# Dealing the edge-count steps of a GNN kernel out anew between the units of its first two dense passes

## What is computed

```
agg  = segment_sum(h[src], dst)              # for every node: sum over its incoming edges
mean = agg / max(deg, 1)
out  = h @ W_self + mean @ W_neigh + b       # relu after the first layer
```

## Time and profile before

| | us |
|---|---|
| median of 3 runs | 1588.9 |
| lowest, highest | 1588.17, 1589.18 |
| the profiled execution, whole | 1588.72 |
| its span, first to last instruction | 1586.6 |
| TensorE busy (matmul) | 1574.5 (99%) |
| VectorE busy | 868.7 (55%) |
| ScalarE busy | 438.6 (28%) |
| GpSimd busy | 140.1 (9%) |

### The profile page before, as it was taken

One profiled execution on the slowest core, in us unless ns is written; L12 is line 12 of the kernel. 1 busy time (PEld: TensorE's weight loads), 2 busy tenths in 40 slices (PEclk: granted clock), 3 DMA queues, 4 the chain that ended last, 5 costly groups with the idle time before them and its releaser, 6 DMA issues.

```text
span 1586.6 us, 22947 instructions
## 1 busy us (share of the span) xinstructions
PE 1574.5 (99%) x7718; PEld 1332.5 (84%) x7720; DVE 868.7 (55%) x1601; ACT 438.6 (28%) x780; POOL 140.1 (9%) x278
## 2 busy tenths in 40 slices
PE   8999999999999999999999999999999999999998
PEld 7777777888888888889989899898998888888886
DVE  8677766464014124564434334343343788888868
ACT  3336554121102001122313123131231233333256
POOL 1351377000000000010000000000001000000000
PEclk9999999999999999999999999999999999999999
DMA  8323344685335545576203012021122333333222
GB/s 305 132 97 134 116 154 161 239 292 206 111 107 182 186 173 183 175 231 236 80 27 106 31 75 79 26 106 34 71 79 106 107 119 119 119 119 119 95 91 50
DMA packets 55974, 205.44 MB, mean 129 GB/s; under 512 B 5392, under 2 KB 14110, under 8 KB 50372
## 3 DMA queue, kind: packets, MB, share of 16 engines
q1 hardware_dynamic: 53204, 190.71, 34.0%
q0 software_dynamic: 2688, 13.63, 2.5%
HBM read 153.85 MB, written 51.52 MB: 129 GB/s over the span
## 4 chain that ended last, share of the span: by engine, by line
PE 95%; DVE 2%; issue 1%; DMA 1%; ACT 0%; SPq 0%; DVEq 0%; ACTq 0%
PE bank L1632 27%; PE bank L1765 27%; PE bank L1784 25%; PE bank L1714 11%; PE bank L1562 2%; PE bank L1606 2%; PE bank L1822 1%; DVE lif_a L1523 0%; DVE w L1259 0%; DMA w_raw<-w_neigh 0%; DMA w_landing<-w_self 0%; DVE lif_b L1523 0%; DMA pr_raw<-w_proj 0%; DVE y L1503 0%; DVE lif_c L1516 0%
## 5 line engine op out<-in xcount | busy, mean ns | idle before, releaser
L1632 PE MATMUL bank<-w,xt 128*128 128x512 f32 x1920 | 467.1, 396 | 0.7 <-DVE xt L1247 0.6
L1765 PE MATMUL bank<-x2t,fc_w 128*128 128x384 f32 (+1 forms) x2304 | 438.4, 350 | 0.6 <-ACT relu L1019 0.6
L1765 PEld LDWEIGHTS bank<-x2t,fc_w 128*128 128x128 f32 x2304 | 411.7, 188 | 25.8 <-issue 0.9
L1632 PEld LDWEIGHTS bank<-w,xt 128*128 128x128 f32 x1920 | 351.9, 188 | 69.8 <-DVE xt L1247 0.8
L1784 PE MATMUL bank<-pr_w,hid 128*128 128x512 f32 (+1 forms) x1728 | 394.8, 389 | 0.0
L1784 PEld LDWEIGHTS bank<-pr_w,hid 128*128 128x128 f32 (+1 forms) x1728 | 320.6, 186 | 70.8
L1473 DVE TENSOR_TENSOR y<-y,bank 128x512 f32<-128x512 f32 (+1 forms) x144 | 98.7, 686 | 207.0 <-PE bank L1784 207.0
L1014 ACT ACTIVATE pr_w<-pr_raw 128x1024 fp32r<-128x1024 f32 x64 | 67.1, 1049 | 366.2 <-PE bank L1784 363.0
L1714 PE MATMUL bank<-z,at 128*128 128x512 f32 x720 | 168.4, 392 | 0.0
L1714 PEld LDWEIGHTS bank<-z,at 128*128 128x128 f32 x720 | 133.9, 188 | 27.3
L1416 DVE TENSOR_TENSOR square<-relu 128x384 f32<-128x384 f32 (+1 forms) x96 | 56.8, 592 | 144.2 <-ACT relu L1019 144.2
(11 more groups left out here) (156 smaller groups left out, 1026.7 us busy)
## 6 DMA issues: line engine op xcount, KB each, us to landing
fc_raw<-w_fc SPq DMA_DIRECT2D x64, 512.0 KB, 4.3
pr_raw<-w_proj SPq DMA_DIRECT2D x64, 512.0 KB, 3.5
xt<-xt_dram SPq DMA_DIRECT2D x24, 1024.0 KB, 5.0
xt_dram<-xt SPq DMA_DIRECT2D x18, 1024.0 KB, 4.4
at<-at_dram SPq DMA_DIRECT2D x18, 640.0 KB, 6.0
part_dram<-rows SPq DMA_DIRECT2D x20, 512.0 KB, 4.0
rows<-part_dram SPq DMA_DIRECT2D x20, 512.0 KB, 4.3
rows<-x SPq DMA_DIRECT2D x17, 512.0 KB, 5.1
```

The lines of the kernel that those rows point to most:

```text
L1632: ins = nc.tensor.matmul(bank[:, 2 * (u % 2) + q, :], xt[j][:, a, k, :], w[:, k, b, q * HALF:(q + 1) * HALF], start=(k == 0 and m == 0), s ...
L1765: ins = nc.tensor.matmul(bank[:, 4 + (c if g == 0 else j % 2), 0:n], fc_w[:, j % 2, k, a, :], x2t[g][:, k, v, c0:c0 + n], start=(k == 0 an ...
```

## The change

The number of steps per unit and their first product are changed, and the third count store's place.

```diff
-A0_STORES = (6, 7, 9)
+A0_STORES = (6, 7, 8)
...
-        [(A0 + 3, 1, 30, 12)] + [(A0 + n, 5, 12, 36) for n in range(4, TILES - 1)] + [(A0 + 9, 3, 12, 24), (S0, 3, 36, 12)]
-        + [(S0 + p, 7 if p in (4, 6, 8) else 8, 0, 48) for p in range(1, TILES)]):
+        [(A0 + 3, 1, 30, 12)] + [(A0 + n, 6, 9, 39) for n in range(4, TILES - 1)] + [(A0 + 9, 5, 9, 35)]
+        + [(S0 + p, 8 if p in (2, 9) else 7, 0, 48) for p in range(1, TILES)]):
```

## The result

| | before | after |
|---|---|---|
| median of 11 runs, us | 1588.71 | 1592.82 |
| lowest, highest | 1587.35, 1589.66 | 1591.65, 1593.62 |
| profiled execution, whole | 1588.72 | 1591.65 |
| its span | 1586.6 | 1589.5 |
| G0's first product, from the span's start | 279.14 | 282.19 |

The ratio of the times is 1.0026, 95% interval [1.0019, 1.0034]: slower by 4.1 us, where 1.4 us was forecast and 0.91 was given to a change under 3.2 us. The measured time lies outside the range of 1587.9 to 1592.1. The profiled execution shows 2.9 of the 4.1.

The account below looks back on a forecast made before the run. TensorE, busy 99% of the span, was taken as the bound, so only its work and waits count. -0.74 + 0.75 + 1.7 - 0.3 = +1.4 us gave 1590.3 us, range 1587.9 to 1592.1 (own range 1589.0 to 1591.5).

Parts of the forecast that it names:

- Light units, +0.75: A0+4 to A0+7, second step at product 15: VectorE's one-hots come late, waits of 0.15 and three of 0.2 us.
- The rival that named reads in A0: Range reads at product 28 of light units collide with 1 MB stores: +3.5 us, 1593.8; chance 0.06.
- A0+8, +1.7: A0+8, second hot step at product 15: TensorE waits 1.7 us for VectorE's one-hots; bounds 0 and 2.5.
- S0's first step, -0.74: S0: the 0.74 us wait for one-hots behind VectorE's last low half of W_self goes.
- A0+9 and the weights, 0: A0+9 into S0: W_self slices still come in time, costing nothing, with 1.35 us of margin.
- Reads in S0, -0.3: S0+5 to S0+7: waits behind slow register reads fall from 1.55 to 1.30 us, about -0.3.
- Steps cost the same wherever they stand: A0 and S0: step prices don't depend on the distance between steps; their sum changes by zero.
- nothing behind G0's start changes: Stages after G0's start keep their lengths; G0's start moves by the forecast sum.
- signs of being wrong: VectorE finishing before product 15 of A0+8, or a difference in a stage behind G0's start.
- the 0.1 to 0.3 named for A0+5 to A0+7: Sign expected if right: TensorE idle 0.1 to 0.3 us ahead of product 15 in these units.

Follow-up runs that it names:

- hot_at_22: Changed kernel with range reads ahead of the step's waits and A0+8's steps before products 9, 22, 28, 34, 40, 46: 1588.60 us, ratio 1.0002.
- keys_first: Changed kernel with early range reads and, from A0+4, the second step's one-hots made before the next tile's rows' low half: 1587.38 us, ratio 0.9994.
- two_in_s0: Changed kernel with three steps in A0+9 and two again in S0 (products 36, 42): 1592.87 us, ratio 1.0031.
- the second profile: The changed kernel unaltered, run once more for another profile: 1592.69 us.

## Why the prediction was wrong, step by step

- **Light units, +0.75: wrong, and this is the step that failed.** "Now it comes at product 15: 15 x 0.229 + 0.88 + 0.27 = 4.59", against one-hots "ready at 4.79". Both times came out (4.6 and 4.83). The step asked only when the one-hots are ready. It left out that an even window's range read stands on TensorE's queue behind the wait for the head keys, and that in each light unit the step at product 15 is an even window. The slack before was not 0.83 but 0.4: in the kernel before's A0+8 the keys come at 119.15, the read runs from 119.32 to 119.65, and the loop's branch ends at 119.98. The last head product could have followed at about 120.04 and came at 120.46. The place moved 0.92 ahead and the keys came 0.22 later: 0.92 + 0.22 - 0.42 = 0.72, and 0.70 was measured in A0+7; in A0+4 to A0+6 the read took 0.6 and not 0.33. Measured 3.78. With the read moved away 1.63 is left, with an odd window 1.32; so 2.1 to 2.5 is the read. The rest is late keys and one-hots with the loop's arithmetic and branch behind them, about twice the forecast; windows with two loop chunks wait 0.6 and not 0.2.
- **The read had been seen, and priced in the wrong stage.** The prediction read the earlier trace rows as a matter of slow transfers in S0 and took reads of 0.333 as free in A0. The rival that named reads in A0 put them at product 28, with the worst length. Product 28 shows no wait: one of the four reads there was slow (0.92, in A0+5), and its lead of 1.3 covered it. Nor does each light unit store 1 MB, as the rival has it: the last such store is issued at 95.04, in A0+6. The reads that cost were of 0.33 and 0.60, at product 15. That the time came near that rival's 1593.8 is luck: it came by another mechanism.
- **A0+8, +1.7: right in kind and nearly in size.** 1.07 at product 15 and 0.36 at the transposes, 1.43. hot_at_22 and keys_first remove the 1.07 in two different ways. The 0.36 was not foreseen: the transposes of tile 9 wait for norm 9 itself, which ended at U + 1.63 (forecast 1.80).
- **S0's first step, -0.74: right.** The wait is gone, and two_in_s0 brings 0.44 of it back.
- **A0+9 and the weights, 0: right.** The margin was 1.7 (forecast 1.35).
- **Reads in S0, -0.3: right in sign, too small.** 1.99 (the small ones counted) fell to 0.56 or 1.03. S0+7, priced at 0.65, costs 0 and 0.20; S0+5 costs 0.27 and 0.41. The prediction looked at the third step of S0+5 to S0+7 alone: S0+8 waited 0.36 at product 20 before and, with the same steps, nothing and 0.13 after; S0+9's third step is an even window too, and S0+4 got a new 0.18. Such waits can't be priced to half a microsecond from one profile. This error of -1.1 hid a part of the +3.0 in the light units.
- **Steps cost the same wherever they stand: right,** to 0.2 us by the 214.6 to 215.0 above, as is that nothing behind G0's start changes.
- **The sum:** -0.74 + 3.78 + 1.43 - 0.07 - 1.43 = 2.97 in the profile, where 1.4 was forecast. Of the medians' 4.1 this leaves 1.1 that no profile shows. The profiled execution was the fastest run of the changed kernel both times. The 1.1 isn't explained. The waits in A0 repeat too well for it. What does vary is the start of A0's first unit, 9.6 to 11.6 us into the span over the thirteen profiles, ahead of everything that the edits touch. That this stretch holds the 1.1 isn't shown, since only one execution of each run is profiled.
- **What the signs missed.** None of the prediction's signs of being wrong appeared. They watched A0+8 and the stages behind G0's start. Only the 0.1 to 0.3 named for A0+5 to A0+7, where 0.96, 0.96 and 0.70 stand, points at the failed step.

## What to carry to other kernels

When work is moved earlier on a queue, the time at which it is wanted is not that of the first big operation but that of the first item in its own chain, and register reads, range arithmetic and branches behind a wait belong to that chain. Look at whether such a read stands behind a wait that it doesn't need: moving it ahead of the wait took a few lines, gave the kernel before 1.6 us, and in the changed kernel hid a read that itself took 1.56. And when several engines follow a written-out order, the item that has just lost its slack should be put ahead of one that still has some.

## What the hardware showed that was not expected

- An open wait on TensorE's queue held back the register read behind it, though the array had earlier products to do for another microsecond (keys at 119.15, read at 119.3, head product at 120.31).
- The same four-register read took 0.33 us, and up to 1.59 in the kernel before and 1.63 in `keys_first`. From A0+4 on, the reads over 0.45 started 1.1 to 7.9 us into a unit in the profiles of the two kernels. In the changed kernel's A0+4 to A0+6 it took 0.60 at 4.7 us, 0.7 behind the issue of a store of 1 MB (65.57, 80.44 and 95.04), again in the second profile, and 0.33 at the same place in A0+7, which has no such store. That the store is the cause isn't shown.
- The half microsecond and more that such a read costs is put down to "issue" on the array (0.27 in A0+7) and to VectorE's one-hots on the weight loads (3.4 in five times). Neither names the read.
